# Transformer expert loop: second product behind head 6, query split on GpSimd, output emptied by ScalarE; five and six weight sets in two sorted stages

## The reference, cut to what matters

```python
x = x + _L1_ffn_ref(_layernorm(x)[None], ...)[0]   # block 3: shared and routed experts
...
x = x + _L2_ffn_ref(_layernorm(x)[None], ...)[0]   # block 5: 8 transformer experts, 2 for each token
...
x = x + _L3_ffn_ref(_layernorm(x)[None], ...)[0]   # block 7: 8 normalised experts, 2 for each token

def _expert(x, Wqkv, ...):                         # one transformer expert, 8 heads of 32 features
    q, k, v = split(x @ Wqkv.T + bqkv, 3)
    attn = softmax(einsum('bhqd,bhkd->bhqk', q * scale, k))
    ctx = einsum('bhqk,bhkd->bhqd', attn, v) @ Wo.T + bo
    x = _layernorm(x + ctx, g1, be1)
    h = gelu(x @ W1.T + bf1); h = gelu(h @ W2.T + bf2)
    return _layernorm(x + h, g2, be2)
# one normalised expert: layernorm(relu(x @ W1 + b1) @ W2 + b2) * gamma + beta
```

## Time and profile before

| | |
|---|---|
| median of 3 runs | 3437.53 us (3427.68 to 3438.13) |
| the profiled execution | 3433.94 us |
| its span, first to last instruction | 3432.2 us |
| TensorE busy | 2519.3 us, 73% |
| VectorE busy | 1643.4 us, 48% |
| ScalarE busy | 1102.1 us, 32% |
| GpSimd busy | 522.7 us, 15% |

### The profile page before, as it was taken

The page is one execution under the profiler, slowest core; times in us unless marked ns, Lnnn a source line. Parts: engine busy times, 40 slices in busy tenths (PEclk is TensorE's granted clock), DMA queues, the critical chain, the costliest instruction groups (busy, mean ns, idle before and its releaser), DMA issues. The chain is left out here.

```text
span 3432.2 us, 53128 instructions
## 1 busy us (share of the span) xinstructions
PE 2519.3 (73%) x18781; PEld 2109.8 (61%) x18781; DVE 1643.4 (48%) x3169; ACT 1102.1 (32%) x2154; POOL 522.7 (15%) x805
## 2 busy tenths in 40 slices
PE   6978698599676687549688888888888885433334
PEld 4867597599466356438567777777777774333323
DVE  3646322322366311334377777777777774333113
ACT  2333121122133111012155555555555552231100
POOL 0000122122121015000001111111111112002112
PEclk9999699699798799769899999999999997666655
DMA  4000122243310027216634114424444201202231
GB/s 114 1 7 1 55 86 86 68 134 98 90 65 25 25 101 250 49 35 247 245 97 109 58 35 115 117 63 108 130 115 131 77 23 38 50 1 96 89 98 64
DMA packets 145018, 291.44 MB, mean 85 GB/s; under 512 B 36146, under 2 KB 73048, under 8 KB 141684
## 3 DMA queue, kind: packets, MB, share of 16 engines
q1 hardware_dynamic: 124532, 231.40, 21.9%
q0 software_dynamic: 20224, 56.65, 6.1%
HBM read 496.49 MB, written 65.74 MB: 164 GB/s over the span
## 5 line engine op out<-in xcount | busy, mean ns | idle before, releaser
L2215 PE MATMUL tx_ring<-g_ident,tx_p 128*128 128x128 f32 x2552 | 427.3, 299 | 128.6 <-issue 45.4
L2215 PEld LDWEIGHTS tx_ring<-g_ident,tx_p 128*128 128x128 f32 x2552 | 315.5, 151 | 222.9 <-issue 63.6
L2434 DVE TENSOR_REDUCE tx_neg_max<-tx_scores 128x1 f32<-128x1354 f32 x232 | 362.2, 1561 | 28.1 <-PE tx_scores L2203 28.1
L2441 DVE COPY tx_p_t<-tx_ring 128x512 f32<-128x512 f32 x464 | 306.9, 687 | 135.5 <-PE tx_ring L2215 130.1
L2341 ACT ACTIVATE tx_p<-tx_scores,tx_neg_max 128x1354 f32<-128x1354 f32 x232 | 322.3, 1389 | 77.1 <-DVE tx_neg_max L2434 76.8
L2203 PE MATMUL tx_scores<-tx_keys,tx_queries 96*128 96x512 f32 (+1 forms) x696 | 222.4, 432 | 13.7 <-DMA tx_queries<-tx_q_hi 11.3
L2348 ACT ACTIVATE tx_p_t<-tx_ring 128x384 f32<-128x384 f32 x232 | 113.4, 489 | 357.8 <-PE tx_ring L2215 356.7
L2753 PE MATMUL nee_wide<-nee_xg_t,nee_w 128*128 128x128 f32 x232 | 55.3, 414 | 156.6 <-issue 156.6
L2254 PE MATMUL tx_ring<-tx_p_t,tx_values 128*32 128x128 f32 x5104 | 151.3, 274 | 21.2 <-ACT tx_p_t L2348 20.8
L2254 PEld LDWEIGHTS tx_ring<-tx_p_t,tx_values 128*32 128x32 f32 x5104 | 135.8, 110 | 34.7 <-ACT tx_p_t L2348 34.0
L2753 PEld LDWEIGHTS nee_wide<-nee_xg_t,nee_w 128*128 128x128 f32 x232 | 48.2, 308 | 165.3 <-issue 165.3
(11 more groups left out here) (907 smaller groups left out, 5430.6 us busy)
## 6 DMA issues: line engine op xcount, KB each, us to landing
tx_keys<-expert_keys SPq DMA_DIRECT2D x696, 169.5 KB
lv1e_w<-in_L_ffn_W SPq DMA_DIRECT2D x232, 256.0 KB
tx_w<-in_L_ffn_W SPq DMA_DIRECT2D x58, 1024.0 KB
lv0e_w<-in_L_ffn_W SPq DMA_DIRECT2D x200, 256.0 KB
tx_values<-expert_values SPq DMA_DIRECT2D x58, 704.0 KB
tx_rows<-in_L_ffn_rows SPq DMA_DIRECT2D x29, 640.0 KB, 3.7
g_adj_t<-in_adj_t POOLq DMA_DIRECT2D x4, 3872.0 KB, 23.1
sro_we<-_L_ffn_expert_out_weight SPq DMA_DIRECT2D x29, 512.0 KB
```

The source lines that it names most:

```text
L2215: last = nc.tensor.transpose(ring[u % 2][:, (t - t0) * P:(t - t0 + 1) * P], p[n % 2][:, t * P:(t + 1) * P], g.ident[:])
L2434: nc.vector.tensor_reduce(neg_max[:, n % 4:n % 4 + 1], sc[n % 2][:, 0:N], AX_X, ALU.max, negate=True)\
L2441: nc.vector.tensor_copy(p_t[:, n % TURNED, t0:t0 + nt, :], ring[u % 2][:, 0:nt * P].rearrange("p (t q) -> p t q", q=P))\
```

## The change

- `SETS` goes from 3 to 6 and `ROUTED_SETS` from 3 to 5.
- In the transformer loop TensorE does `second(i - 1)` behind head 6 instead of head 7, and in head 6 it does `scores(n + 2)` ahead of piece 1 instead of behind it. VectorE does `add_second` at head 6.
- `split_queries` moves from VectorE to GpSimd, behind `middle_rows` and ahead of the next `fetch`.
- The output product is emptied by ScalarE (`keep_output`), ahead of `keep_rows`; VectorE then adds the residual from SBUF.
- `mix` waits for piece 2 of its last head only before its ninth block of keys.

```diff
-ROUTED_SETS = 3
+ROUTED_SETS = 5
...
-             5: ("first0", "first1"), 7: ("second",)}
+             5: ("first0", "first1"), 6: ("second",)}
...
-                  "values0": "dve", "values1": "dve", "output": "dve", "second": "dve"}
+                  "values0": "dve", "values1": "dve", "output": "act", "second": "dve"}
...
-                for c in (1, 2):
-                    written(pe, at["heads", i, (4 * half + 3, c)])
+                written(pe, at["heads", i, (4 * half + 3, 1)])
                 for t in range(NB):
+                    if t == TG[2][0]:
+                        written(pe, at["heads", i, (4 * half + 3, 2)])
...
                         turn(i, hd, 0)
-                        turn(i, hd, 1)
+                        if hd != 6:
+                            turn(i, hd, 1)
                         if HEADS * i + hd + AHEAD < heads:
                             scores(HEADS * i + hd + AHEAD)
+                        if hd == 6:
+                            turn(i, hd, 1)
                         turn(i, hd, 2)
...
-                    if hd == 7 and i:
+                    if hd == 6 and i:
                         second(i - 1)
...
+            def keep_output(i):
+                u = at["output", i, 0]
+                act.wait_ge(full, u + 1)
+                if i:
+                    act.wait_ge(x1_n_done, i)
+                nc.scalar.activation(x1[:], ring[u % 2][:, 0:D], ACT.Copy).then_inc(drained["act"], 1)
...
-                u = at["output", i, 0]
-                dve.wait_ge(full, u + 1)
+                written(dve, at["output", i, 0])
                 dve.wait_ge(residual, i + 1)
-                nc.vector.tensor_tensor(x1[:], ring[u % 2][:, 0:D], x_res[:, i % 2, :], ALU.add).then_inc(drained["dve"], 1)
-                written(dve, u)
+                link(nc.vector.tensor_tensor(x1[:], x1[:], x_res[:, i % 2, :], ALU.add))
...
+            def split_queries(i):
+                written(pool, at["queries", i, 0])
+                pool.wait_ge(q_done, i + 1)
+                if i:
+                    pool.wait_ge(q_stacked, 16 * 12 * i)
+                own(nc.gpsimd.tensor_copy(q_hi[:], q[:]))
+                nc.gpsimd.tensor_tensor(q_lo[:], q[:], q_hi[:], ALU.subtract).then_inc(q_split, 1)
...
-SETS = 3
+SETS = 6
```

More of the change, by code:

```diff
@@ L2410, in _ @@
                         keep_inverse(i - 1, 1)
-                    if hd == 1 and i + 1 < tiles:
-                        keep_rows(i + 1)
+                    if hd == 1:
+                        if 0 < i <= tiles:
+                            keep_output(i - 1)
+                        if i + 1 < tiles:
+                            keep_rows(i + 1)
                     if hd == 2 and i + 1 < tiles:
@@ L2449, in scale_bias @@
                     .then_inc(q_scaled, 1)
-            def split_queries(i):
-                written(dve, at["queries", i, 0])
-                dve.wait_ge(q_done, i + 1)
-                if i:
-                    dve.wait_ge(q_stacked, 16 * 12 * i)
-                link(nc.vector.tensor_copy(q_hi[:], q[:]))
-                nc.vector.tensor_tensor(q_lo[:], q[:], q_hi[:], ALU.subtract).then_inc(q_split, 1)
             def inverse(i, half):
@@ L2525, in _ @@
             scale_bias(0)
-            split_queries(0)
             row_max(0)
@@ L2545, in _ @@
                             middle_norm(i - 1)
-                        if i + 1 < tiles:
-                            split_queries(i + 1)
                     if hd == 3 and i < tiles:
@@ L2551, in _ @@
                         context(i, 0)
-                    if hd == 6 and i >= 2:
-                        end_stats(i - 2)
+                    if hd == 6:
+                        if i >= 2:
+                            end_stats(i - 2)
+                        if 0 < i <= tiles:
+                            add_second(i - 1)
                     if hd == 7:
@@ L2558, in _ @@
                             inverse(i, 1)
-                        if 0 < i <= tiles:
-                            add_second(i - 1)
             back.mix(dve, spare)
@@ L2612, in _ @@
                 fetch(i)
+            split_queries(0)
             for i in range(tiles + 2):
@@ L2618, in _ @@
                     middle_rows(i - 1)
+                if i + 1 < tiles:
+                    split_queries(i + 1)
                 if i + 2 < tiles:
```

## The result

The changed kernel takes **3198.57 us** (median of 4 runs, 3197.28 to 3202.82), the kernel before in the same session 3435.57. The ratio is 0.9316, with a 95% interval of 0.9298 to 0.9334: 237 us less, where 203 were forecast, and inside the range of 3190 to 3285. The profiled execution has a span of 3200.6 us.

The account below looks back on a forecast made before the run. Relays between engines bound the transformer loop and, through late loads, the normalised stage. Savings of 166 (normalised) + 0 (routed) + 39 (loop) - 2 (prologue and tail) = 203 us from 3437.5 gave 3235 us, range 3190 to 3285.

Parts of the forecast that it names:

- Normalised stage: Six sets let loads start three tiles earlier and hide: 28 intervals go from 260.9 to 95.0 us, saving 166 us.
- Second product: Transformer loop, behind head 6: the 1.53 us stall moves behind VectorE's chain as 1.4; a full-clock tile gains 0.2 us.
- Columns late: Transformer loop: later end_norm delays scale_bias and context, so head 1's copies and TensorE wait, costing 0.4 us a tile.
- Split: Transformer loop: moving the query split to GpSimd frees VectorE of 1.75 us and gains 1.15 us between mix and mix.
- Margin of the queries: Transformer loop: the slack before scores need the split queries shrinks from about 5 us to 0.3 to 1.3.
- Clock: Transformer loop: 0.6 of the 1.68 us a mean tile loses to lowered clock comes back, 17 us in all.
- Loop: Transformer loop: 22 us over 28 full-clock tiles, 38.07 to 37.27 us each, plus 17 us of clock, together 39 us.
- (1): Transformer loop gains under 10 us, as query copies land late or the clock falls in mix: 3270 us, chance 0.16.
- (2): Normalised stage: loads slowed by their own traffic, 4.8 us a tile, 24 us less gain: 3259 us, chance 0.12.
- (4): Transformer loop: GpSimd's split makes queries late, 28 us per us over the margin; slower than before, chance 0.01.
- (5): Normalised stage: the 6.96 us idle does not end at the weights, so only the loop counts: 3400 us, chance 0.02.
- (3): More than forecast: the clock returns in full and normalised tiles run at 2.88 us: 3191 us, chance 0.07.

Follow-up runs that it names:

- the undone kernel: The changed kernel with the second product and its bias back behind head 7 and head 6's scores behind piece 1 again: 3210.61 us.

## Why the prediction was right, and where its sizes were off

- **Normalised stage, 166 us.** Right: 171.9 by first products in the profile, 173 alone. The load over the output of three tiles before was the relay. The forecast had 20 intervals at 3.6 us and 8 at 2.88; the trace has 19 at 3.52 and nine at 2.46. That the 3.6 came so near is in part luck: it was chosen between 3.27 and 4.3 as a matter of DMA traffic alone, and the second limit, SyncE's four issues of a set, was wrongly dismissed with "stand ahead of only the bias table". Undisturbed they take 3.21 us of a tile's 3.49 in the middle.
- **Routed stage, 0.** Right, within 8 us.
- **Second product, 0.2 us.** The mechanism is right: a stall of 1.29 released by VectorE (1.4 forecast), the 0.80 and 1.53 gone. The gain is smaller still: `mix` at 16.63 (16.5 forecast, 16.64 before), and the undone kernel gives 0.04. That the move changes where and how often the clock falls was left in the clock's term.
- **Columns late, 0.4.** The mechanism is there, 1.77 us of idle time before `scale_bias`, but in the full-clock tile shown `context` would have been due only 0.1 us earlier: 0.1. In three tiles it cost 0.5 to 0.8. `scale_bias` itself ran 5.3 us behind the norm's end (5.5 forecast); what I added for TensorE's restart did not occur.
- **Split, 1.15 us.** Under-sized: 1.51. Without VectorE's 1.75 us the stall of 1.16 went, but "0.4 each" for what is late next was too much; one wait of 0.30 came (2361.70). GpSimd needs 0.39 + 0.73, less than the 1.5 I took, and its subtraction does not meet the copy of the inverse (0.23 at 2362.51), so the 0.15 for it fell away too. With these three sizes and the second product's, the forecast of 37.27 becomes 37.27 - 0.36 - 0.15 - 0.3 + 0.16 = 36.62, as measured.
- **Margin of the queries.** In one of 27 tiles the scores waited 0.47 us; the margin had been put at 0.3 to 1.3.
- **Output and values.** Nothing, as said for the second, though the 0.41 us stall that was to stay became 0.20; the first had been counted inside the 15.7.
- **Clock, 0.6 of 1.68 us a tile.** 37.40 - 36.62 = 0.78 is left, so 0.9 came back.
- **Loop.** 39 forecast, 60 by first products. The forecast took its 1.4 us a tile times 28; measured were 2.3 us a tile over 26 tiles and nothing over the last two. The missing part of a tile is 0.65 us at full clock (0.83 more than forecast between the two `mix`: split 0.36, contention 0.15, columns 0.3; 0.19 less ahead of the first) and 0.3 of clock.

Of the 34 us by which the result beats the forecast, 21 are the loop and 6 the normalised stage. The rest is the 2 for prologue and tail, which no row shows, and what medians and profiled executions differ by. So the direction and both mechanisms were right, and the sizes of the loop's terms were too small.

The rivals: (1) appeared in part, as `mix` partly at half clock in 12 of 27 tiles (4.0 to 4.3 us instead of 2.61, not twice as long), but not with its price. (2), (4) and (5) did not occur. (3) came nearest, with a total of 3199 against its 3191.

## What to carry to other kernels

When more buffers take a wait away, count the issues of one round on the issuing engine, not only the bytes: with four issues to a set SyncE needed 3.21 us undisturbed, and the tiles took 3.49. And take a round's length from rounds, not from a stage's mean: 9.32 was the mean of a stage whose rounds took 11.2, and the forecast for four sets failed by it. An engine's chain that has just taken over a stall is worth reading for what stands in it by accident: moving the last norm away, and with it GpSimd's work beside the copy, gave the changed kernel 37 us, clock included and with the columns loaded earlier. And two variants equal at full clock (36.62 and 36.66) can differ by the clock: by 5 us in the loop here, with the stalls in other places.

## What the runs showed of the hardware

- A stall of 1.29 us once a tile, with shorter ones near it, went with a fall to 1.2 GHz in 12 of 27 tiles; at 0.42 us in its place it fell only behind a stall of 4.19 us elsewhere, which made 2 slow tiles. When it falls in `mix`, 88 small products take 4.10 us instead of 2.61.
- GpSimd's elementwise work beside VectorE costs VectorE by what it runs, not by its being busy: a 128x128 copy from SBUF took 0.77 instead of 0.23, copies out of PSUM of 128x512 stayed at 0.69 or less.
- The issue of an indirect scatter on GpSimd (1.10 us) held up a VectorE product of PSUM and SBUF for 1.0 us in 26 of 27 tiles, when it came due 0.38 us into the issue; a product that started 0.35 us into it was not late, and with the scatter behind it there was no delay either. The Trainium skill, DMA: Bandwidth & Descriptors, SWDGE vs HWDGE vs iDMA, says that VectorE in its two-port mode keeps GpSimd out of the memory where GpSimd writes its descriptors. Here it went the other way: the issue ran its usual 1.10 us and VectorE was late.
- A cast of 128x256 to fp32r takes 0.39 us on GpSimd, and 0.85 on VectorE in its usual place; the subtraction 0.73 on GpSimd and 0.91 on VectorE there. VectorE's fastest cast, 0.294, shows that this is its place and not its speed.
